# A fused attention and mixture-of-experts kernel: two batches' attention work interleaved step by step

## The reference

```python
x = x + tanh(g_xattn) * xattn(layernorm(x), ctx, ctx, Wq, bq, Wk, bk, Wv, bv, Wo, bo)
x = x + tanh(g_ffn) * moe(layernorm(x), Wr, br, W1, b1, W2, b2)
# xattn: scores = q k^T / 4 for each head, softmax, times v, times Wo, plus bo
# moe:   logits = xt @ Wr + br; the two largest; softmax over the two;
#        out = sum of gate * (relu(xt @ W1[e] + b1[e]) @ W2[e] + b2[e])
```

## Time and profile before

| | |
|---|---|
| median of 3 runs | 1002.23 us (1001.48 to 1002.8) |
| profiled execution, its own time | 1005.98 us |
| its span, first to last instruction | 1004.1 us |
| mean granted TensorE clock | 0.92 |
| PE busy over the span | 832.2 us, 83% |
| DVE | 616.5 us, 61% |
| ACT | 441.6 us, 44% |
| POOL | 377.5 us, 38% |
| DMA packets, bytes | 104171, 98.81 MB |

### The profile page before, as it was taken

How to read it: one execution, slowest core, us unless ns; L and a number is a source line. 1 busy time by engine, 2 the same in 40 slices (tenths; PEclk the granted TensorE clock), 3 DMA queues, 4 the chain that set the end, 5 groups by cost and what they waited for, 6 DMA issues and landing times.

```text
span 1004.1 us, 21736 instructions
## 1 busy us (share of the span) xinstructions
PE 832.2 (83%) x6483; PEld 542.1 (54%) x6484; DVE 616.5 (61%) x1107; ACT 441.6 (44%) x777; POOL 377.5 (38%) x365
## 2 busy tenths in 40 slices
PE   4788889888888888985047999999999999999920
PEld 3344444444444444433026777777777777777710
DVE  3567666666677677662994556555555655655557
ACT  3456665666666766432503333333333333333300
POOL 2113323333233333102513355555555655555210
PEclk9799998999999999976557999999999999999975
DMA  4324443444444344212451111111111111111159
GB/s 133 101 76 144 130 147 123 144 147 144 139 139 133 119 129 129 61 56 100 134 185 44 42 49 52 47 47 52 47 47 48 51 42 52 47 47 49 36 197 326
DMA packets 104171, 98.81 MB, mean 98 GB/s; under 512 B 9478, under 2 KB 96972, under 8 KB 104012
## 3 DMA queue, kind: packets, MB, share of 16 engines
q1 hardware_dynamic: 92140, 73.75, 23.5%
q0 software_dynamic: 7488, 20.46, 6.7%
q10 hardware_dynamic: 4512, 4.20, 1.2%
HBM read 67.03 MB, written 31.20 MB: 98 GB/s over the span
## 4 chain that ended last, share of the span: by engine, by line
PE 63%; DVE 17%; issue 7%; ACT 4%; DMA 4%; SPq 3%; POOL 1%; DVEq 0%; ACTq 0%; POOLq 0%
PE banks L1359 19%; PE banks L1345 7%; PE banks L1346 7%; PE banks L1347 7%; PE banks L1104 6%; DVE negmax L851 5%; PE banks L1223 3%; PE banks L1203 3%; ACT probs L706 3%; PE banks L1087 3%; PE banks L1161 2%; DVE stats L790 2%; DVE hot_col L986 2%; PE banks L1332 2%; PE banks L1240 1%
## 5 line engine op out<-in xcount | busy, mean ns | idle before, releaser
L1359 PE MATMUL banks<-wall,hh 128*128 x624 | 222.7, 379 | 0.5 <-DVE yb L1038 0.5
L752 ACT ACTIVATE hid<-banks,b_col 128x256 f32<-128x256 f32 x312 | 130.8, 470 | 209.8 <-PE banks L1347 114.2
L851 DVE TENSOR_REDUCE negmax<-banks 128x4 f32<-128x1024 f32 x128 | 155.6, 1218 | 49.5 <-PE banks L1161 48.0
L1345 PE MATMUL banks<-xh,wall 128*128 128x256 f16 x624 | 171.2, 274 | 0.0
L1346 PE MATMUL banks<-xl,wall 128*128 128x256 f16 x624 | 171.1, 274 | 0.0
L1347 PE MATMUL banks<-xh,wall 128*128 128x256 f16 x624 | 171.1, 274 | 0.0
L592 POOL DMA_INDIRECT y_rows<-yb,dest_idx x78 | 106.7, 1368 | 162.7 <-DVE yb L1038 125.5
L1359 PE MATMUL banks<-wall,hl 128*128 x624 | 157.3, 273 | 0.0
L706 ACT ACTIVATE probs<-banks 128x1024 f32<-128x1024 f32 x128 | 125.8, 1023 | 38.7 <-PE banks L1188 38.4
L1036 DVE SCALAR_TENSOR_TENSOR yb<-banks,b_b 128x256 f32<-128x256 f32 x78 | 33.1, 425 | 133.0 <-PE banks L1359 133.0
L1030 DVE TENSOR_TENSOR hl<-hid,hh 128x1024 f16<-128x1024 f32 x78 | 95.6, 1225 | 2.7
(11 more groups left out here) (159 smaller groups left out, 1242.9 us busy)
## 6 DMA issues: line engine op xcount, KB each, us to landing
wst<-in_L_ffn_W SPq DMA_DIRECT2D x32, 512.0 KB, 5.6
ks<-k_parts SPq DMA_DIRECT2D x96, 64.0 KB, 2.4
qs<-q_parts SPq DMA_DIRECT2D x96, 64.0 KB, 2.4
xin<-in_x SPq DMA_DIRECT2D x16, 256.0 KB, 3.2
cin<-in_ctx SPq DMA_DIRECT2D x16, 256.0 KB, 3.8
k_parts<-kparts SPq DMA_DIRECT2D x16, 256.0 KB, 2.3
q_parts<-qparts SPq DMA_DIRECT2D x16, 256.0 KB, 2.3
xres<-in_x SPq DMA_DIRECT2D x16, 256.0 KB, 2.8
```

The costliest lines, as they stand in the source:

```text
L752: ins = nc.scalar.activation(hid[half][:, c % (HC // 2), :], banks[:, b, c % 2 * TS:(c % 2 + 1) * TS], ACT.Relu, bias=b1_col[:, ds(e * HC ...
L851: nc.vector.tensor_reduce(negmax[:, c, 8 * (g // 2):8 * (g // 2) + 8].rearrange("p (m g p2) -> p m g p2", m=2, g=2)[:, :, g % 2, :], banks ...
L1345: nc.tensor.matmul(dst, hi, xh[par][:, m, :], start=(m == 0), stop=False)
L1359: ins = nc.tensor.matmul(dst, h_[:, c, s * P:(s + 1) * P], w_, start=(c == 0 and k == 0), stop=(c == HC - 1 and k == 1))
```

## The change

Body m now runs the **attention pass of m-1 beside the max pass of m**, in eight steps u. A step is: block u of `scores` of m-1, block u of `scores_max` of m, one portion of other work, block u of `attend` of m-1. Post is that of m-2, the projections `k` and `q` are of m+1, `v` is of m, and the turns are of m+2. There are 18 bodies for 16 batches: body 0 has no attention pass, body 16 has only the attention pass and post, body 17 only post. Bodies 0 to 3 and 14 to 17 are written out, 4 to 13 are the loop. With it:

- Banks: the max pass has banks 0 and 1 and the scores banks 2 and 3, one pair each instead of two alternating ones. Each block waits for the reader of the block before. Bank 4 serves in turn k, q, v and the turned x; banks 5 and 6 the other turns, `output` and the router; bank 7 the attended values, one group at a time.
- ACT: no more float32 copies of q and k (the factor 16 is put into `wk` and `wq` once, by DVE, at the start). New on ACT: `max_row` and the copies to `oT`. Gone from ACT: the scaling of the weights.
- DVE: the low halves of q and k, straight from PSUM. Gone from DVE: both normalizations, the adding of epsilon, `max_row`, the `oT` copies.
- POOL: the normalizations, the epsilon, the scaling of the weights in place. Gone: the cuts of q and k.
- SP: `load_part` in two halves of four heads, 24 DMAs of 32 KB a batch for 12 of 64 KB. Store k, store q, first halves, first max row, results; then, in the next body, x, second halves, second max row, residual, weights.
- A second `ctxT` and `stats` buffer, and a separate `x2T`.
- The late weights: pieces 0 and 1 load at the end of body 15; pieces 0 to 5 are cut in bodies 16 and 17, 6 and 7 behind them. POOL makes all of them before the iota constants on which routing waits.

```diff
@@ SP: load_part
-                wait(sp, st_done, 8 * (n - 1))
+                wait(sp, st_done, 8 * (n - 2) + 4 * (h + 1))
...
-                        sp.dma_start(dst[par][a:a + DH, :, :],
+                        sp.dma_start(dst[par][a:a + DH, 4 * h:4 * h + 4, :],
@@ POOL: body
                 if post:
-                    residual(n - 1)
...
+                    residual(m - 2)
+                if last >= 0:
+                    late_low(3 * last)
+                if turns:
+                    norm1(m + 2, par)
+                if post:
+                    norm2(m - 2)
+                if last >= 0:
+                    late_low(1 + 3 * last)
+                    late_low(2 + 3 * last)
                 if weights:
                     for w in range(2):
+                        hold(pool, w_hi, 2 * (2 * (t - 1) + par) + w + 1)
+                        nc.gpsimd.tensor_scalar(wst[w][:], wst[w][:], WSCALE, None, ALU.mult).then_inc(w_scaled, 1)
@@ PE: scores_max, scores, attend
-                wait(pe, mx_red, 8 * n + w - 1)
+                wait(pe, mx_red, 8 * n + w)
...
-                if v_ >= 2:
-                    pe.wait_ge(exp_done, 8 * n + v_ - 1)
+                wait(pe, exp_done, 8 * n + v_)
...
-                if c == 0 and g >= 2:
-                    pe.wait_ge(av_evac, 4 * n + g - 1)
+                if c == 0:
+                    wait(pe, av_evac, 4 * n + g)
@@ DVE: low_part, in place of POOL's cut
+                dve.wait_ge(evac, n + 1)
+                for m in range(M):
+                    ins = nc.vector.scalar_tensor_tensor(out=parts_[:, 1, m, :], in0=banks[:, 4, m * L:(m + 1) * L],
+                                                         scalar=qk_col[:, which, m:m + 1], in1=parts_[:, 0, m, :],
+                                                         op0=ALU.add, op1=ALU.subtract)
@@ PE: body
+                for u in range(8):
+                    if attention:
+                        scores(m - 1, 1 - par, u)
+                    if maxima:
+                        scores_max(m, par, u)
...
+                    if attention:
+                        attend(m - 1, 1 - par, u)
+                    if u == 7 and post:
+                        router(m - 2, turns, maxima)
```

More of the change, by code:

```diff
@@ L306, in wait, with within, parts_of @@
             hold(eng, s, v) if eng.engine in HOLDS else eng.wait_ge(s, v)
+        LEAD = 4
         def bodies(eng, body):
[L311 to L317, removed]
+            for m in range(LEAD):
+                body(m // 2, m % 2)
+            with eng.Fori(LEAD // 2, NB // 2 - 1) as t:
+                body(t, 0)
+                body(t, 1)
+            for m in range(NB - 2, NB + 2):
+                body(m // 2, m % 2)
+        def within(m, first, last):
+            return not isinstance(m, int) or first <= m <= last
+        def parts_of(m):
+            maxima = within(m, 0, NB - 1)
+            ahead = within(m, 0, NB - 2)
+            turns = within(m, 0, NB - 3)
+            attention = within(m, 1, NB)
+            post = within(m, 2, NB + 1)
+            weights = within(m, 2, 2 * W_KEPT + 1)
+            return maxima, ahead, turns, attention, post, weights
         assert NB // 2 - 2 == W_KEPT
@@ L730, in _ @@
+            bodies(act, body)
+            for i in range(6, len(LATE)):
                 late_high(i)
@@ L903, in _ @@
-            PER_BODY = 2 + 2 + 2
-            body(0, 0, False, 2)
-            body(0, 1, False, 2)
-            with dve.Fori(1, NB // 2 - 1) as t:
-                chain[1] = (t - 1) * (2 * PER_BODY)
+                    if w == 1 and ahead:
+                        k_low(m + 1)
+                    if maxima:
+                        reduce(m, w)
+                    if w == 1 and post:
+                        attended(m - 2, 0)
+                        attended(m - 2, 1)
+                    elif w == 2:
+                        if turns:
+                            norm1_stats(m + 2, t + 1, par)
+                    elif w == 3:
+                        if ahead:
+                            q_low(m + 1)
+                    elif w == 4 and post:
+                        residual(m - 2)
+                        norm2_stats(m - 2)
+                    elif w == 7 and post:
+                        router(m - 2)
@@ L913, in _ @@
-            body(NB // 2 - 1, 0, False, 1)
-            body(NB // 2 - 1, 1, False, 0)
-            attended(NB - 1, 0)
-            attended(NB - 1, 1)
-            residual(NB - 1)
-            norm2_stats(NB - 1)
-            norm2(NB - 1)
-            router(NB - 1)
+            chain[0], chain[1] = was + (NB // 2 - 1 - LEAD // 2) * 2 * PER_BODY, 0
+            for m in range(NB - 2, NB + 2):
+                body(m // 2, m % 2)
             dve.wait_ge(iota_ready, 1)
```

624 lines of the change are left out of this document (300 added, 324 removed).

## The result

The forecast was 972 us, with 0.90 on faster. Measured: **1007.57 us** (1006.33 to 1009.8, six runs) beside 1002.51 for the kernel before (1001.1 to 1006.25), ratio 1.0043 [1.0026, 1.006]. Measured again beside the later experiments, the same kernel gave 1005.31 beside 1005.24, ratio 1.0018 [0.9998, 1.0037]. So the change costs 0.2 to 0.4%, the first of the two just clear of nothing and the second not, and the 30 us that were to be gained are missing.

What follows compares the result with a forecast made beforehand. PE was taken to bound the kernel, with gains possible only in attention and just behind it: bodies from 27.0 to 24.0 us. Attention -29.2, tail +12.2, routing -13.0 make -30 us: 972 us, range 956 to 990.

Steps and rivals of the forecast that it cites:

- The walk of the period: Loop body: eight steps counted one by one give 23.7 us, plus 0.3 for register waits, 24.0 us a body.
- 23.1 to 25.5: Bounds on a loop body in us: PE's own work below, each step giving up another 0.2 us above.
- the cover of 2.0 us: q's trip through DRAM: row of maxima there at 22.0 us of the body, needed at 24.0.
- near 17 us and some 3 of waits: SP's own work in a loop body, issuing 37 DMAs where it issued 25.
- The slower rival: q loop through SP sets the period, q's store landing behind the weights: body 27.0, whole 1008 us; chance 0.07.
- deciding point, 26.5 a body: Body length from which the slower rival decides, since 12 x 2.5 us has then eaten the 30 us gain.
- the tail: After attention: last normalization ends 13.5 us on, then POOL's late pieces and iotas; routing starts at 30.0, +12.2 us.
- The rival of 25.2 a body: Loop bodies lose another 1.2 us to SP's loop or DVE's small steps: 986 us; chance 0.2.
- The price of GpSimd's scaling: POOL's multiplication of a weight piece by a constant: 1.5 us, between 0.92 and 2.14; a late piece 3.6.
- Attention's end: Attention ends at 427.9 us where it ended at 457.1, with twelve loop bodies at 24.0: -29.2 us.
- Routing alone: Routing without POOL work beside it, so DVE's instructions no longer stretch: -13.0 us, bounds 0 and 13.
- The first max block: Start of the kernel: first max block at 34.0 us for 27.8, as k waits for scaled weights: +6.2.

Runs made afterwards that it cites:

- k_first: Changed kernel with SP storing k of batch m+1 ahead of the body's weight loads instead of after them; 981.4 us, ratio 0.9764 to the kernel before.
- act_scales: Changed kernel with the scaling of all weight pieces moved from POOL back to ACT, POOL only subtracting; 999.48 us, ratio 0.9962 to the kernel before.
- late_dve: Changed kernel with the low halves of the eight late weight pieces made by DVE in one instruction each, none by POOL; 987.46 us, ratio 0.985.
- the experiment start: Changed kernel with DVE scaling weights before the second statistics and SP loading batch 0's first halves before its second halves; 999.26 us, ratio 0.9954.

## Why the prediction was wrong, point by point

**The walk of the period held.** Its steps and the rows agree but for step 0, whose k runs at the half clock: exponentials every 2.1 to 3.0 us from step 1 to step 7, a normalization covered in most bodies, maxima that hold a max block for 0.2 us at most. With the order of the stores mended the loop's bodies take 23.3 us (k's stores of k_first at 162.19 and 371.79, nine apart), inside 23.1 to 25.5, and attention ends at 427.97, for 427.9 forecast. That this agrees to a tenth is luck: bodies 2 to 13 begin at 78.22 and end at 362.96, 3.3 us less than forecast, and the late start (+1.9) and bodies 14 to 16 (+1.4) make it up.

**The step that failed is the cover of 2.0 us.** It began at q's low half, 12.3 us into the body, added q's store 0.4, and let the twelve loads follow. The store's landing was left out, and that the first six loads are k's, which need k's store, not q's. In the rows k's store is issued 11.0 us into the body, behind SP's other work and the weights; its landing ends at 16.9, not 12.7; loads 5.6; the row is issued by 23.9 and TensorE goes on at 25.1, for a row that I had there at 22.0. The cover of 2.0 was a debt. The same landing is missing from the other count, that of SP's own work: "near 17 us and some 3 of waits", 20 of 24. In eight rounds of the changed kernel (k's stores at 165.31 and 367.79) the issues take 17.0 us each, as forecast, and 8.3 lie between them, 5.1 of these from k's store to the first load behind it (the stores' own issues not counted). That makes 25.3, the body as measured. I had taken the landing of 2.3 from the earlier trace rows, where nothing as large was in the queue ahead of the store. That the row moved by three microseconds is thus one unpriced landing, 4.2 us later, less a microsecond by which waits and the last landing came out shorter than forecast.

**The rivals.** The slower rival named this place, SP's queue with a store behind the weights, and a body of 27.0; it was the mechanism, with k's store in q's place and 25.3 instead of 27.0, and I gave it 0.07. Its deciding point, 26.5 a body, was right only while the tail held: the tail's own error brought it down. The Trainium skill (DMA: Bandwidth & Descriptors, Rules for kernel authors) would have many small transfers made one, and no run here shows what that would be worth. The half loads land in 1.8 us (64 KB took 2.3, so halving did shorten the landing) and cost 0.45 each as forecast, but the twelve more of them are 5.4 us of SP's round, and no run joined the halves again. The rival of 25.2 a body had the body right, but with its tail as forecast it gave 986 us.

**The price of GpSimd's scaling** was 2.78 us, above the upper bound of 2.14 that I took from the subtraction with two inputs. Fewer inputs do not make it cheaper. The Trainium skill (GPSIMD Engine Reference, Engine selection) calls one-input work on GpSimd roughly line rate; the price by that, which I estimated at 1.1 us, was further off. In the loop, with SP as the pace, it cost nothing that act_scales could recover; in the tail it made the late piece 4.9 for 3.6.

**The sum, by its terms.** Attention's end: bodies 2 to 13 12 x 1.33 = +16.0; their start at 78.2 for 76.3, +1.9; bodies 14 to 16 +5.3, most of it in body 16, which late_dve shortens by 2.9. Together +23.2. The tail: the last normalization ends 17.9 behind the end of attention for 13.5, +4.4, since piece 3 at the new price is still running when the variance is there; pieces 4 to 7 and the iotas 21.3 for 16.5, +4.8. Routing alone gave back 12.6 for 13.0, the one term with a proof in the rows of before. -30 + 23.2 + 9.2 + 0.4 = +3, and the first expert starts 2.8 us later than before (537.68 for 534.89). The first max block, 34.0 for 34.0, was exact, and the experiment start shows what it was worth.

## What to carry to other kernels

When a step is to be hidden behind others, follow its data through the queue that carries it: what is issued ahead, how long the landing takes with that in flight, and which later issue waits for which landing; a landing time read from a quiet queue is not its price behind a megabyte. And when an engine's rows show a wait and a slow stretch behind it, fill the wait before calling it the cause, and look at the other engines' rounds: here the clock came back in most bodies and the time did not, and SP's rows had the same round as before. Sum up the queue's own round, issues and landings, as one does an engine's busy time. An order of issues is one line, and was worth 24 to 26 us of 1007.

## What the hardware did that was not expected

- GpSimd multiplies 128x1024 f32 by a constant in 2.78 us and subtracts two such tiles in 2.13; VectorE does both in one instruction of 1.21.
- A 256 KB store lands in 3.0, 4.2 or 5.7 us with 0, 0.5 or 1 MB of loads issued just ahead in its queue, and in 4.6 with the megabyte in another engine's queue.
- TensorE's k products, 1.89 us for eight at 2.4 GHz, took up to 3.62 behind a wait of 1 to 3 us, which is 1.2 GHz; the granted clock of the stretch from 231 to 234 us was 0.50, of most others near it 1.00; with the wait filled by products they took 1.89 in 8 of 14 bodies (3 of 14 without). The time did not fall with it.
